# Layer-1 self-attention of a four-layer decoder: per-group loop replaced by one unrolled pipeline of eight-head units

## What is computed

```python
def L1_attn(x, Wq, bq, Wk, bk, Wv, bv, Wo, bo, gamma, beta):
    q = einsum('bsd,dhk->bshk', x, Wq) + bq       # h = 16 heads, k = 64
    k = einsum('bsd,dhk->bshk', x, Wk) + bk
    v = einsum('bsd,dhk->bshk', x, Wv) + bv
    attn = softmax(einsum('bqhk,bshk->bhqs', q, k) / 8, axis=-1)
    ctx = einsum('bhqs,bshk->bqhk', attn, v)
    y = x + einsum('bqhk,hkd->bqd', ctx, Wo) + bo
    return (y - mean(y)) * rsqrt(var(y) + 1e-3) * gamma + beta
x = x + L1_attn(layernorm(x), ...)
```

## Time and profile before

| | us |
|---|---|
| median of three runs | 2171.47 |
| the profiled execution | 2183.54 |
| its span, first to last instruction | 2181.8 |

### The profile page before, as it was taken

How to read it: one execution, slowest core, us unless ns; L and a number is a source line. 1 busy time by engine, 2 the same in 40 slices (tenths; PEclk the granted TensorE clock), 3 DMA queues, 4 the chain that set the end, 5 groups by cost and what they waited for, 6 DMA issues and landing times.

```text
span 2181.8 us, 28588 instructions
## 1 busy us (share of the span) xinstructions
PE 1469.7 (67%) x9264; PEld 1057.7 (48%) x9264; DVE 1326.0 (61%) x3654; ACT 802.7 (37%) x1241; POOL 166.2 (8%) x128
## 2 busy tenths in 40 slices
PE   5978979785268888878963398879798930000465
PEld 3967968453237567563542277745565510000344
DVE  4444444687865556546777745367576348988445
ACT  4354453464233443434644322146443420000122
POOL 2000000221000000002211100022000000000001
PEclk9999999897689999988995569579799965555568
DMA  3000000200000000000000000000000120000000
GB/s 102 1 0 0 0 1 27 102 6 1 0 0 1 0 0 0 5 0 10 6 6 1 0 0 0 0 11 6 1 1 0 32 94 1 1 1 27 21 10 20
DMA packets 19276, 26.95 MB, mean 12 GB/s; under 512 B 3184, under 2 KB 14448, under 8 KB 18288
## 3 DMA queue, kind: packets, MB, share of 16 engines
q1 hardware_dynamic: 19184, 25.84, 3.5%
HBM read 20.33 MB, written 5.51 MB: 12 GB/s over the span
## 4 chain that ended last, share of the span: by engine, by line
PE 39%; issue 34%; DVE 17%; ACT 6%; POOL 2%; DVEq 1%; DMA 0%; SPq 0%; POOLq 0%; ACTq 0%
PE PSA L750 3%; PE PSA L760 3%; PE PSA L566 3%; PE PSA L601 3%; PE PSA L568 2%; PE PSA L942 2%; PE PSA L1023 2%; DVE W L1969 2%; DVE W L1958 2%; PE PSA L959 2%; PE PSA L686 2%; DVE BIG L1962 2%; PE PSA L581 2%; DVE BIG L1965 2%; ACT W L420 1%
## 5 line engine op out<-in xcount | busy, mean ns | idle before, releaser
L1050 PE MATMUL PSA<-W,TMP 128*128 128x128 f32 x32 | 8.3, 441 | 266.1 <-DVE TMP L1994 266.1
L1461 DVE TENSOR_REDUCE MX<-PSA 128x4 f32<-128x512 f32 x128 | 88.3, 690 | 143.5 <-PE PSA L568 94.0
L490 POOL TENSOR_TENSOR RSTD<-VEPS,HALF 128x4 f32<-128x4 f32 x50 | 50.7, 1013 | 1228.5 <-DVE VEPS L1434 1228.5
L750 PE MATMUL PSA<-BIG 32*128 32x512 f32 x384 | 117.4, 712 | 36.6 <-POOL BIG L496 19.5
L1215 ACT ACTIVATE QK<-PSA 128x512 f32<-128x512 f32 x192 | 105.0, 595 | 98.7 <-PE PSA L760 98.7
L1560 DVE TENSOR_REDUCE MX<-PSA 128x8 f32<-128x1024 f32 x96 | 116.7, 1216 | 34.3 <-PE PSA L750 33.7
L1050 PEld LDWEIGHTS PSA<-W,TMP 128*128 128x128 f32 x32 | 7.1, 327 | 267.3 <-DVE TMP L1994 267.3
L760 PEld LDWEIGHTS PSA<-K,BIG 128*128 128x128 f32 x768 | 90.5, 148 | 80.1 <-ACT BIG L1208 65.2
L1208 ACT ACTIVATE BIG<-BIG 128x1024 f32<-128x1024 f32 x96 | 101.7, 1060 | 59.6 <-DVE BIG L1564 59.5
L1564 DVE TENSOR_TENSOR BIG<-PSA,MX 128x1024 f32<-128x1024 f32 x96 | 117.5, 1224 | 8.2 <-PE PSA L760 5.1
L760 PE MATMUL PSA<-K,BIG 128*128 128x128 f32 x768 | 111.0, 291 | 13.9 <-ACT BIG L1208 13.3
(11 more groups left out here) (331 smaller groups left out, 3656.4 us busy)
## 6 DMA issues: line engine op xcount, KB each, us to landing
CTX<-in_ctx_t SPq DMA_DIRECT2D x16, 256.0 KB, 3.0
W<-in_w SPq DMA_DIRECT2D x1, 2048.0 KB, 7.3
ROWS<-in_rows SPq DMA_DIRECT2D x1, 1744.0 KB, 13.2
W<-in_w SPq DMA_DIRECT2D x2, 768.0 KB, 5.5
W<-in_w SPq DMA_DIRECT2D x1, 1412.0 KB, 12.3
W<-in_w SPq DMA_DIRECT2D x2, 512.0 KB, 11.0
scratch_q<-BIG SPq DMA_DIRECT2D x4, 256.0 KB, 2.4
scratch_k<-BIG SPq DMA_DIRECT2D x4, 256.0 KB, 2.8
```

The costliest lines, as they stand in the source:

```text
L750: mm = pe.matmul(banks[n], QN[r, it % 2, tok(i)], KM[r, it % 2, i].rearrange("p r t -> p (r t)"), start=p != "L1x", stop=True, skip_group_ ...
L1461: dve.tensor_reduce(MX[:, tok(u % 4, 4)], tile(PS[1 + u % 3]), AX_X, ALU.max).then_inc(max_taken.sem, 1)
```

## The change

`L1a` becomes one unrolled pipeline over 32 units of eight heads (`m`; a sequence has two, `n = m // 2 - 1` is the sequence whose output is made), like the cross-attention phases. Keys and queries are kept for two pairs of sequences (`K1`, `Q1`, each `[128, pair % 2, 8, 256]`) without zeros. Scores are 64-row matmuls of one head each, alternating between partitions 0 to 63 and 64 to 127 and between two banks. Maximum, subtraction and exponential take 128 x 1024. Transposes all go through bank 4, products through bank 5, and projections, output transposes and output projection share banks 6 and 7. Projections of pair + 2 are made between the units of a pair. The value bias is no longer added to `V1`; since the softmax weights sum to one, `bv` goes through the output weights once and is added to `bo` (BVB, eight small matmuls). ACT now copies the values, DVE the queries. The zeroing ahead of `L0f` is gone, that ahead of `L1f` stays. The post-norm is split and placed in units 0 and 1 of the next group.

```diff
@@ layout
-        K1 = BIG[:, 0:8192].rearrange("p (c b r t) -> p c b r t", c=8, b=GB, r=2)
+        K1 = BIG[:, 0:4096].rearrange("p (n c t) -> p n c t", n=2, c=8)
+        Q1 = BIG[:, 4096:8192].rearrange("p (n c t) -> p n c t", n=2, c=8)
@@ gpsimd
-                if p in ("L0f", "L1f") and p != run[0]:
+                if p == "L1f" and p != run[0]:
 
                     pool.wait_ge(x_updated.sem, x_updated.before[p])
                     pool.memset(BIG[:, 0:8192], 0.0).then_inc(kd_zero, 1)
@@ tensor, scores of a unit
-                    for n in range(2):
-                        c = 2 * g + n
-                        mm = pe.matmul(bank[:, tok(n, 256)], Q1[:, c, tok(i)], K1[:, c, i].rearrange("p r t -> p (r t)"),
-                                       start=True, stop=True)
+                    if m >= 2:
+                        pe.wait_ge(shifted.sem, shifted.at(p, 0, m - 2))
+                    for x in range(4):
+                        for r in range(2):
+                            half = slice(64 * r, 64 * r + 64)
+                            mm = pe.matmul(PS[2 * (m % 2) + r][:, tok(x)], Q1[half, pair % 2, 4 * h + x, tok(s)],
+                                           K1[half, pair % 2, 4 * h + x, tok(s)], start=True, stop=True)
@@ tensor, loop
+                for m in range(total):
+                    pair, q, n = m // 4, m % 4, m // 2 - 1
+                    done, first, second = m >= 2 and m % 2 == 0, pair + 1 < total // 4, pair + 2 < total // 4
+                    if m + 3 < total:
+                        scores(m + 3)
+                    if m + 1 < total:
+                        transposes(m + 1, 0)
+                    product(m, 0)
+                    if q == 0 and first:
+                        values(pair + 1, 2, 6)
+                    if q == 1 and second:
+                        keys(pair + 2, 0, 6)
+                        queries(pair + 2, 0, 7)
+                    if q == 2 and second:
+                        keys(pair + 2, 2, 6)
+                    if q == 3 and second:
+                        keys(pair + 2, 3, 6)
+                        queries(pair + 2, 3, 7)
+                    if done:
+                        outputs(n, 0, 7)
+                    if m + 1 < total:
+                        transposes(m + 1, 1)
+                    if q == 1 and second:
+                        keys(pair + 2, 1, 6)
+                    if q == 3 and second:
+                        values(pair + 2, 0, 6)
+                    if done:
+                        outputs(n, 1, 6)
+                    product(m, 1)
...
+                    if done:
+                        project(n, 6)
@@ vector, loop
+                def shift(m):
+                    dve.wait_ge(max_taken.sem, max_taken.at(p, 0, m))
+                    if m >= 2:
+                        dve.wait_ge(t_psum.sem, t_psum.at(p, 0, 2 * (m - 2) + 1))
+                    dve.tensor_tensor(tile(PH1[:, m % 2, :], 8), scores_of(m), last(high(m), P), ALU.subtract).then_inc(shifted.sem, 1)
...
+                    if m + 3 < total:
+                        take_max(m + 3)
+                    normalise(m, 0)
...
+                    if m + 3 < total:
+                        shift(m + 3)
+                    normalise(m, 1)
...
+                    if e == 0 and it:
+                        post_stats(it - 1)
+                    if e == 1 and it:
+                        post_update(it - 1)
+                    if e == 6 and it + 1 < GROUPS:
+                        next_moments(p, it + 1)
+                    if e == 7 and it + 1 < GROUPS:
+                        next_normed(p, it + 1)
```

More of the change, by code:

```diff
@@ L94 @@
 R_AT, R_ALL = sections([
[1 row of a table removed]
+    ("L1a.bo", 128), ("L1a.gamma", 128), ("L1a.beta", 128),
     ("L1x.bv", 128), ("L1x.bo", 128), ("L1f.b1", 512), ("L1f.b2", 128),
@@ L285, in decoder @@
         each = lambda names, n=1: {p: n for p in names}
-        attention = (*SMALL, "L1a")
+        attention = SMALL
         cross = lambda n: each(CROSS3, n)
@@ L317, in decoder @@
         v_ready = signal("v_ready", {**each(SMALL), "L1a": 8, **cross(1)})
-        units = {**each(attention, GB * HG), **cross(HALVES)}
+        units = {**each(attention, GB * HG), "L1a": HALVES, **cross(HALVES)}
         units2 = {**units, "L2a": GB * 2}
-        quarters = {**units, **cross(2 * HALVES)}
+        quarters = {**units, "L1a": 2 * HALVES, **cross(2 * HALVES)}
         s1_psum = signal("s1_psum", units)
@@ L410, in kd_zeroed @@
         def kd_zeroed(p):
-            return sum(q in run[1:run.index(p) + 1] for q in ("L0f", "L1f"))
+            return sum(q in run[1:run.index(p) + 1] for q in ("L1f",))
         def strip_of(j):
@@ L516, in _ @@
                         pool.wait_ge(x_updated.sem, x_updated.before["L1a"])
-                    pool.memset(V1[:, :, :, 64:65], 1.0).then_inc(setup_pool, 1)
+                    pool.memset(V1[:, :, :, :, 64:65], 1.0).then_inc(setup_pool, 1)
+                    ln_root(p, 0)
+                    for it in range(GROUPS - 1):
+                        ln_root(p, it + 1)
+                        root(p, it, 0)
+                    root(p, GROUPS - 1, 0)
+                    continue
                 if p in before_loop:
@@ L587, in product_v @@
                 pe.wait_ge(p_ready.sem, p_ready.at(p, it, u))
-                if p == "L1a":
-                    if u >= 2:
-                        pe.wait_ge(on_ready.sem, on_ready.at(p, it, u - 2))
-                elif g == 0 and i >= 2:
+                if g == 0 and i >= 2:
                     pe.wait_ge(on_ready.sem, on_ready.at(p, it, i - 2))
@@ L1092, in relu_ffn @@
                 transpose_next(p, it)
-            bodies = {"L1a": l1_attention, "L0f": bit_ffn, "L1f": bit_ffn, "L2a": linear_attention,
+            bodies = {"L0f": bit_ffn, "L1f": bit_ffn, "L2a": linear_attention,
                       "L2f": experts, "L3o": delta_out, "L3x": one_head, "L3f": relu_ffn}
@@ L1110, in _ @@
                     transpose_next(p, BEFORE_LOOP)
+                if p == "L1a":
+                    l1_attention(p)
+                    continue
                 if p == "L3a":
@@ L1136, in xnt_next @@
                 act.wait_ge(xnt_psum.sem, xnt_psum.at(p, it))
-                act.activation(XNT[:], PS[7 if p in CROSS3 and it is not BEFORE_LOOP else XNT_BANK.get(p, 2)], ACT.Copy).then_inc(xnt_ready.sem, 1)
+                act.activation(XNT[:], PS[7 if p in (*CROSS3, "L1a") and it is not BEFORE_LOOP else XNT_BANK.get(p, 2)], ACT.Copy).then_inc(xnt_ready.sem, 1)
             def exponentials(p, it, scale):
@@ L1151, in exponentials @@
                     act.activation(PR[:, u % 2, :], PS[4 + u % 2], ACT.Copy).then_inc(p_ready.sem, 1)
-                    if p == "L1a" and u >= 5 and u % HG == 1:
-                        outputs_t(p, it, (u - 5) // HG)
                     if u == UNITS - 3:
                         xnt_next(p, it)
-                if p == "L1a":
-                    outputs_t(p, it, GB - 1)
-            def outputs_t(p, it, i):
-                for half in range(2):
-                    act.wait_ge(ot_psum.sem, ot_psum.at(p, it, 2 * i + half))
-                    act.activation(OT1[:, 4 * half:4 * half + 4, :], tile(PS[0]), ACT.Copy).then_inc(ot_ready.sem, 1)
             def keys(p, new, g):
@@ L1381, in _ @@
                         scan(it)
-                if p in ("L1a", "L2a") and kd_zeroed(p):
+                if p == "L2a" and kd_zeroed(p):
                     act.wait_ge(kd_zero, kd_zeroed(p))
@@ L1497, in attend @@
                         next_normed(p, it)
-                if fill:
-                    fill()
-                if norm:
-                    norm(p, it, GB - 1)
-                else:
-                    for u in range(UNITS - 3, UNITS):
-                        norm_unit(u)
-                    take_y(GB - 2)
-                    take_y(GB - 1)
+                norm(p, it, GB - 1)
             def values(p, new):
@@ L2173, in lay_out @@
     c["lane"] = (np.arange(P)[:, None] // HD % 4 == np.arange(4)[None, :]).astype(np.float32)
+    c["L1a.bv"] = a["L1_attn_bv"].reshape(8, P).T
     for n in "qk":
```

364 lines of the change are left out of this document (276 added, 88 removed), and 1 row of the table W_PHASE.

## The result

The changed kernel takes 2109.05 us (median of 4 runs, 2107.2 to 2111.45), the kernel before, with a run on the same chip added, 2177.76 (4 runs, 2169.0 to 2184.85). The ratio is 0.9687, 95% interval 0.964 to 0.9733: faster by 3.1%. The profiled execution has 2111.45, span 2109.7.

The account below looks back on a forecast made before the run. PE was taken to bound `L1a`: work 252.2 plus waits 37.7 makes 289.9 against 350.35, 60.4 us less; with 1.7 in `L0f`, 62 off 2171.5 gives 2110, range 2092 to 2145.

Parts of the forecast that it names:

- the small ones in 24 units: PE's small waits for banks 6 and 7 in `L1a`'s loop: 0.15 in each of 24 units, 4 us.
- those of the last seven units: Units 25 to 31, without projections: PE waits for DVE's normalise of bank 5 and the update, about 1 each, 7 us.
- Scores: In `L1a`, alternating 64-row matmuls run side by side: 1.18 us a unit, 37.8 in all, where 57.6 goes.
- Output tail: `L1a`'s output transposes and projection get other matmuls between them, covering ACT's 0.7 us copy: 22 us paid back.
- Update after e = 1: DVE's post-norm update makes PE's second product in the next unit wait 2.3 us, three times: 7.
- Prologue: Start of `L1a`: key and query copies on two banks, first exponential and copies, lower clock for 3 us: 7 us.
- End: End of `L1a`: last normalise 0.9, two copies 1.6, lower-clock output projection 1.9, final stretch 6.6: 11 us.
- The first: Rival: 64-row score matmuls in `L1a` don't overlap, 2.06 us a unit, 28 more, kernel 2138; chance 0.11.
- the third: Rival: half-row weight loads neither run side by side nor hide, 3.8 us a unit, 84 more, kernel 2194; chance 0.04.
- The second, bank 5: Rival: latency bounds `L1a`'s loop, second product waiting for DVE's normalise; 32 us more, kernel 2142; chance 0.12.
- The fourth: Rival: overlap comes but booked waits in `L1a` (updates, prologue, small ones) don't; up to 18 us less, 2092; chance 0.10.
- The base: Starting time of the whole kernel: 62 us taken off both the profiled 2183.54 (giving 2121.5) and the median 2171.5 (2109.5).

Follow-up runs that it names:

- E3: Changed kernel with a unit's eight score matmuls reordered, four on the upper 64 rows first, then four on the lower; 2105.4 us, `L1a` 307.05.
- E2: Changed kernel with all eight score matmuls of a unit reading partitions 0 to 63 (wrong result); 2144.43 us, `L1a` 317.34.
- E6: Changed kernel with a sequence's output transposes and output projection next to each other again, using bank 6 in turn; 2142.25 us, `L1a` 329.58.
- E4: Changed kernel with POOL zeroing the block-diagonal key buffer ahead of `L0f` again; 2094.09 us.
- E7: Changed kernel with the first exponential ahead of the copies of the second pair of value blocks in `L1a`'s prologue; 2101.86 us, `L1a` 285.07.
- E8: Changed kernel with DVE taking each unit's maximum twice from the fourth unit on; 2115.26 us, `L1a` 297.92.
- c_after: The changed kernel run and profiled once more, as it is; 2117.61 us.
- E5: Changed kernel with DVE's post-norm update in `L1a` cut into four steps, in entries 1 to 4; 2111.55 us, `L1a` 281.56.
- c_before: The kernel before, run and profiled again as it is; 2169.77 us.

## Why the prediction was right, and where it was not

- **The phase.** Forecast 289.9, measured 290.04. So close a match is luck: two errors of 16 cancel. Booked were 252.2 of work and 37.7 of waits. By starts PE works 268.4 and idles 21.3. Work was put too low for the projections (82.6 booked, 92.1 measured: a block steps by 0.92 behind a change of operation where 0.86 was taken, and by up to 1.9 in the prologue), the transposes (28.2, 32.3), the output projections (28.8, 32.8) and the output transposes (14.1, 15.2). Some 7 us of it are matmuls at the lower clock, part of which the prediction had booked among its waits.
- **Waits too high.** Two were put far too high: the small ones in 24 units (4 booked; in the loop at the upper clock there are six of 0.06) and those of the last seven units (7 booked; 0.34, 0.30, 0.30 and 0.42).
- **Scores.** 1.18 a unit forecast, 1.09 measured: 2.9 too much. The step from lines 750 and 772 to a 64-row matmul was right, and E3 shows its reason: neighbours on different strips (and see there on the banks). The transposes behind the scores step by 0.49 (742.33 to 742.83), so changing over costs about 0.05 there and 0.2 inside the 1.09 (8 x 0.11 is 0.88). The Trainium skill (TensorE: Matmul & The Clock Gate, The mechanism) has loads overlap matmuls only when the row group differs. E2 has one row group throughout and steps by 0.124 for load and matmul together, near the 0.11 of an instruction with its load on full rows and far from the 0.22 of the two in turn: the measurement does not bear the rule out in this form.
- **Products.** 0.90 forecast, 0.84 measured for 8 x 0.105: 3.8 too much over 64.
- **Output tail.** Waits of 22 paid back: E6 finds 21.3 of these, and 20 more that the step left out: that a stop costs 0.90 to 0.95 where 0.7 is recorded, the lower clock, and the products' waits. The forecast of the phase did not suffer, since it was built from what remains, not from what goes; but as a price of the old order it was half.
- **Update after e = 1.** 2.3 times 3 forecast. Measured 2.0 (748.20 - 745.68 - 0.49), and 1.5 once for the projection at the lower clock behind it, which E4 does without.
- **Prologue.** 7 booked. The loop begins at 662.24, 34.05 behind the first matmul. By the prediction's prices the work in it is 22 blocks of 0.86, three scores, the bias product 1.8 and two transposes, 25.1; so 8.9 are left. Of these 3.1 are idle; the rest is work dearer than its price, mostly at the lower clock (the first three groups of projections take 1.7 to 1.9 instead of 0.92). The term left out is ACT's table load, 1.28, and the two value copies ahead of the exponential: E7, which takes these copies out of the way, is 3.2 shorter.
- **End.** 11 forecast. The last waits and the last projection at the lower clock:

```profile
902.65 1.08 PE L910 MATMUL PSA<-BIG,QK 128*128 128x65 f32 x8 [0.87 <-DVE QK L1841]
904.59 1.06 PE L919 MATMUL PSA<-K,QK 128*128 128x128 f32 x8 [0.86 <-DVE QK L1841]
906.49 3.37 PE L927 MATMUL PSA<-W,BIG 128*128 128x128 f32 x16 [0.83 <-ACT BIG L1397]
916.48 1.19 PE L719 MATMUL PSA<-CTX,W 128*128 128x512 f32 x1 [6.63 <-issue]
```

  0.86 and 0.83 of waits, 3.37 instead of 1.88, and from 909.9 to the stretch's end at 916.37 another 6.5, beside the 0.87: 10.6.
- **The zeroing.** 1.7 forecast, 1.71 measured, and shown by E4.
- **The rivals.** The first falls by the 1.09, the third by E2, which is as near to it as a kernel here came. The second, bank 5, is not what happens: 8 of 64 products waited, and E8 had to add 33 us to DVE to lose 9.6. The fourth was half right: of 37.7 booked PE idled only 21.3, but its work was longer by as much, so the time it gave did not come.
- **The signs.** The granted clock did not stay at 1.0: it was 0.89 up to 662, 0.76 from 748 to 755, 0.78 from 903 to 909.9, and 1.00 from 700 to 748 and from 755 to 903. Apart from the 6.6 of the end, PE's largest wait was the 3.1 of the prologue, not one after e = 1. And a gain outside `L0f` and `L1a` was named as a sign of being wrong: between the two profiled executions 9.7 of the 72 lie there, and are not the change's.
- **The base.** This is the step that failed. I wrote that the profiled execution was 12 above the median "in which I see no reason to expect other waits", and took the same 62 off both. They differ, if not in waits, by how many loops of `L2a` run at the lower clock. The profiled execution came out at 2111.45 where the sum for it says 2121.5; `L2a` (4.7 less) and the phases behind it (7.8 less) make up for it, `L1x` is 2.7 longer. That the median, 2109.05, met 2110 so closely is luck as well: the medians of the kernel before and the changed one, run beside each other, differ by 68.7, 34.3 and 61.1 in the three comparisons, at the same 62 of the phases. c_after, with three slow loops, has 2117.61, and with none it would be near 2087 (my estimate: 2109.05 less 2 x 11; E4, which has none, is at 2084.66 in its profiled execution). The range of 2092 to 2145 was made of waits in `L1a` alone, and its real width is set as much by this.

## What to carry to other kernels

Put matmuls on half the rows side by side and alternate the halves: the order alone was worth 0.55 of 1.64 us a unit. Between a transpose and the matmul that needs its copy put other matmuls, and price such a wait from start to start, not by its record, where PE is the bound: in the one case tried here it came to twice the record. Judge an edit by the phase it touches, in a profile, when the phases that it does not touch move by more than it can.

## What the runs showed of the hardware that I had not expected

The two clock levels in `L2a`. Ahead of each loop PE does the same projections and waits 2.62 us for DVE. The changed kernel and E4, the first loop of each:

```profile
1198.53 1.98 PE L1041 MATMUL PSA<-XNT,W 128*128 128x512 f32 x4 [0.76 <-DVE QK L2067]
1203.13 3.13 PE L1065 MATMUL PSA<-QK,BIG 128*128 128x128 f32 x16 [2.62 <-DVE QK L2067]
1206.06 1.73 PE L1082 MATMUL PSA<-BIG,PR 128*128 128x16 f32 x8
```
```profile
1198.03 1.98 PE L1041 MATMUL PSA<-XNT,W 128*128 128x512 f32 x4 [0.76 <-DVE QK L2067]
1202.63 2.05 PE L1065 MATMUL PSA<-QK,BIG 128*128 128x128 f32 x16 [2.62 <-DVE QK L2067]
1204.58 1.06 PE L1082 MATMUL PSA<-BIG,PR 128*128 128x16 f32 x8
```

With the same instructions and the same waits of 0.76 and 2.62 ahead of it, one loop is granted 0.55, that is mostly 1.2 GHz, for its 26.7 us, the other the full 2.4 GHz. E4, E5 and E7 differ from the changed kernel only in `L0f` or `L1a`, and have none, three and one such loops; c_before and before, one program, have none and two. All 56 loops of the 14 profiles stand behind a wait of 2.62, and 22 are slow. What decides it was not found; it was only seen that a shift of a few us far ahead goes with another outcome, and that it did not stay the same between executions of one program. The Trainium skill (TensorE: Matmul & The Clock Gate, What's actually happening) says that the chip's look at PE's activity is free-running and not tied to the kernel's start, so that the same kernel gets a different number of slow matmuls from run to run. The two outcomes behind equal waits agree with that; no run here shows the mechanism. So each of these loops has 11 us that hang on something that the code doesn't set. Whether the gap of 2.6 us in front of it is needed for that is not shown; taking it away wasn't tried.

The second: a DVE instruction that starts during POOL's memset of 128 x 8192 took 2.2 us instead of 0.47 and ended with it, in the kernel before and in E4 alike. The instructions of DVE ahead of it run beside the same memset and are not held up: line 1972 takes 1.90 for its three in E4 beside it, and 1.90 in the changed kernel without it. The Trainium skill (SBUF — State Buffer, SBUF: two separate sides) has DVE and GpSimd share a pair of ports as an exclusive lock that some kinds of DVE instruction take, those in a two-port mode among them, and others don't, the loser blocked for the whole of the other's instruction. The 2.2, ending with the memset, agrees.
